# Layer 3 of a four-layer graph network in steps of one whole graph, with its start laid into the end of layer 2

## The reference

```python
Wh = (h @ W).reshape(b, n, H, HD).transpose(0, 2, 1, 3)
e1 = jnp.einsum('bhnd,d->bhn', Wh, a1)
e2 = jnp.einsum('bhnd,d->bhn', Wh, a2)
e = e1[:, :, :, None] + e2[:, :, None, :]
e = jnp.where(adj_mask[:, None, :, :] == 0, -jnp.inf, e)
e = jnp.where(e >= 0, e, ALPHA * e)
attn = jax.nn.softmax(e, axis=-1)
h_prime = jnp.einsum('bhij,bhjd->bhid', attn, Wh)
x = _layernorm(x + h_prime.transpose(0, 2, 1, 3).reshape(b, n, D_OUT))
```

## Time and profile before

| | us |
|---|---|
| median of 3 runs | 810.21 (804.77 to 817.69) |
| the profiled execution's own time | 810.46 |
| its span, first to last instruction | 808.7 |
| busy in the span: PE, DVE, ACT, POOL | 722.9, 651.0, 556.9, 447.4 |

### The profile page before, as it was taken

How to read it: one execution, slowest core, us unless ns; L and a number is a source line. 1 busy time by engine, 2 the same in 40 slices (tenths; PEclk the granted TensorE clock), 3 DMA queues, 4 the chain that set the end, 5 groups by cost and what they waited for, 6 DMA issues and landing times.

```text
span 808.7 us, 18443 instructions
## 1 busy us (share of the span) xinstructions
PE 722.9 (89%) x6397; PEld 507.2 (63%) x6397; DVE 651.0 (81%) x1754; ACT 556.9 (69%) x1141; POOL 447.4 (55%) x534
## 2 busy tenths in 40 slices
PE   3899599999689999999999999869999999999993
...
DMA packets 28893, 14.98 MB, mean 19 GB/s; under 512 B 1920, under 2 KB 28800, under 8 KB 28800
## 3 DMA queue, kind: packets, MB, share of 16 engines
...
## 4 chain that ended last, share of the span: by engine, by line
PE 51%; DVE 26%; issue 9%; ACT 9%; POOL 2%; DVEq 1%; DMA 1%; POOLq 1%; ACTq 0%
PE pair L985 10%; PE pair L1061 8%; PE bank L985 8%; ACT loopm L680 3%; DVE arena L898 3%; DVE ln L534 2%; PE bank L1149 2%; PE bank L1086 2%; DVE nmx L957 2%; PE pair L1164 2%; DVE P L937 2%; PE bank L1051 2%; PE pair L1167 2%; DVE nmx L903 2%; DVE pT L858 2%
## 5 line engine op out<-in xcount | busy, mean ns | idle before, releaser
L583 POOL TENSOR_TENSOR arena<-arena,nmx 128x1024 f32<-128x1024 f32 x64 | 121.4, 1898 | 129.1 <-DVE nmx L903 129.1
L604 POOL TENSOR_TENSOR P<-P,nmx 128x512 f32<-128x512 f32 x128 | 133.2, 1041 | 80.8 <-DVE nmx L957 78.8
L499 POOL TENSOR_TENSOR ln<-ln,neghalf 128x4 f32<-128x4 f32 x64 | 66.3, 1035 | 137.5 <-DVE ln L535 137.5
L741 ACT COPY arena<-pair 128x1024 f32<-128x1024 f32 x64 | 64.8, 1012 | 91.3 <-PE pair L985 91.3
L505 POOL TENSOR_SCALAR X<-yb,ln 128x128 f32<-128x128 f32 x256 | 119.1, 478 | 9.2 <-issue 9.2
L898 DVE TENSOR_TENSOR arena<-pair,mask 128x1024 f32<-128x1024 f32 x64 | 78.3, 1223 | 47.6 <-PE pair L1061 47.6
L937 DVE TENSOR_TENSOR P<-pair,t 128x512 f32<-128x512 f32 x128 | 87.6, 684 | 21.3 <-ACT t L761 21.1
L1061 PE MATMUL pair<-arena,hg 32*128 32x256 f32 x512 | 93.9, 444 | 2.7 <-DVE arena L898 1.7
L761 ACT ACTIVATE t<-pair 128x512 f32<-128x512 f32 x128 | 77.7, 607 | 21.9 <-PE pair L1167 21.7
L957 DVE TENSOR_REDUCE nmx<-P 128x4 f32<-128x512 f32 x128 | 85.8, 670 | 0.8
L765 ACT ACTIVATE P<-P 128x512 f32<-128x512 f32 x128 | 80.9, 632 | 3.9 <-POOL P L604 3.9
...
## 6 DMA issues: line engine op xcount, KB each, us to landing
...
```

The costliest lines, as they stand in the source:

```text
L583: nc.gpsimd.tensor_tensor(v3(P2[t % 3], HEADS), v3(P2[t % 3], HEADS), nmx2[t % 2][:].unsqueeze(2).broadcast_to([128, HEADS, N]), ALU.add)\
L604: nc.gpsimd.tensor_tensor(v3(P[u % 4][:], HQ), v3(P[u % 4][:], HQ), nmx[u % 4][:].unsqueeze(2).broadcast_to([128, HQ, N]), ALU.add)\
```

## The change

Layer 3 becomes `layer3(t)`, one graph per step, in the manner of layer 2. Scores go into `pair[t % 2]`, both banks. Scaling, maximum, reduction, addition of the row maximum, exponential and the copy of the transposes have 1024 columns each; `P`, `pT` and `t3` now lie in layer 2's buffers. The preparation has four steps (transposes of X, e, transposes of e, V) in `early(t)`, one bank; e and V are separate products, and e is split in PSUM without `er`. The addition of X moves from DVE to POOL, ahead of the scales of the batch before. Layer 3's step t stands behind layer 2's step t + 69 on every engine; it begins with t = -5, and the first scores are at t = 0. The product with V (PE) now waits for `L3_on`, the count of DVE's last product.

```diff
-def later_layers(eng, layer1, layer2, layer3, last):
+def later_layers(eng, layer1, layer2, layer3):
 
 
     every_batch(eng, layer1, before=True, after=1)
     for t in range(-4, 0):
         layer2(t)
     layer1(BATCHES + 1, 1, BATCHES // 2)
+    two_layers(layer2, layer3)
+
+
+def two_layers(layer2, layer3):
+
     for t in range(GRAPHS):
         layer2(t)
-    for u in range(UNITS):
-        layer2(GRAPHS + u)
-        layer3(-1, 1, -1, (u,))
-    for u in range(UNITS):
-        layer2(GRAPHS + UNITS + u)
-        layer3(0, 0, 0, (u,))
-    for b in range(1, BATCHES + last):
-        layer3(b, b % 2, b // 2)
+    for t in range(-AHEAD, GRAPHS + BEHIND):
+        layer2(GRAPHS + AHEAD + t)
+        layer3(t)
...
-        pair = [ctx.enter_context(nc.psum_tensor(f"pair{i}", [128, 1024], F32)) for i in range(2)]
-        bank = [pair[i // 2][:, i % 2 * 512:i % 2 * 512 + 512] for i in range(4)]
-        bank += [ctx.enter_context(nc.psum_tensor(f"bank{i}", [128, 512], F32))[:] for i in range(4, 8)]
+        pair = [ctx.enter_context(nc.psum_tensor(f"pair{i}", [128, 1024], F32)) for i in range(4)]
+        bank = [pair[i // 2][:, i % 2 * 512:i % 2 * 512 + 512] for i in range(8)]
...
-        P = [sb(f"P{i}", [128, HQ * N]) for i in range(4)]
-        pT = [sb(f"pT{i}", [128, HQ * N]) for i in range(2)]
-        xw1 = [P[s] for s in range(2)]
-        z1 = [pT[s] for s in range(2)]
+        xw1 = [sb(f"xw1{s}", [128, W]) for s in range(2)]
+        z1 = [sb(f"z1{s}", [128, W]) for s in range(2)]
...
+        t3 = kk
...
-        t3 = [sb(f"t3{i}", [128, HQ * N]) for i in range(2)]
-        nmx = [sb(f"nmx{i}", [128, HQ]) for i in range(4)]
...
-        def out_bank(b):
-            return bank[4] if b < BATCHES - 2 else bank[1]
+        def early(t):
+            return bank[5] if t < 0 else bank[6]
...
+            def layer3(t):
+                if graph(t - 1):
+                    pool.wait_ge(sem("L3_max"), t)
+                    p = P2[(t - 1) % 3]
+                    nc.gpsimd.tensor_tensor(v3(p, HEADS), v3(p, HEADS),
+                                            nmx2[(t - 1) % 2][:].unsqueeze(2).broadcast_to([128, HEADS, N]), ALU.add)\
+                      .then_inc(sem("L3_less_max"), 1)
+                b, j = t // G, t % G
+                if j == 0 and real(b - 2):
+                    pool.wait_ge(sem("L3_on"), G * (b - 1))
+                    nc.gpsimd.tensor_tensor(yb[b % 2][:], yb[b % 2][:], x_of(b - 2), ALU.add).then_inc(sem("L3_y_done"), 1)
+                if j == 3 and real(b - 2):
+                    norm_pow(pool, 3, b - 2, b % 2, b // 2)
+                    norm_scale(3, b - 2, b % 2, (0, 1))
+                if j == 0 and real(b - 3):
+                    norm_scale(3, b - 3, (b - 3) % 2, (2, 3))
+
             every_batch(pool, layer1)
-            for t in range(GRAPHS + UNITS):
-                layer2(t)
-
-            def layer3(b, s, turn):
-                for u in range(UNITS):
-                    if b == 0:
-                        layer2(GRAPHS + UNITS + u)
-                    if real(b):
-
-                        pool.wait_ge(sem("L3_max"), UNITS * b + u + 1)
-                        nc.gpsimd.tensor_tensor(v3(P[u % 4][:], HQ), v3(P[u % 4][:], HQ),
-                                                nmx[u % 4][:].unsqueeze(2).broadcast_to([128, HQ, N]), ALU.add)\
-                          .then_inc(sem("L3_less_max"), 1)
-                    if real(b - 2):
-                        if u == 5:
-                            norm_pow(pool, 3, b - 2, s, turn - 1)
-                        if u >= 6:
-                            norm_scale(3, b - 2, s, (2 * (u - 6), 2 * (u - 6) + 1))
-            every_batch(pool, layer3, after=2)
+            two_layers(layer2, layer3)
...
+            def layer3(t):
+                g = t - 4
+                if graph(g):
+                    act.wait_ge(sem("L3_pT_mm"), g + 1)
+                    need(act, sem("L3_pv_mm"), g - 1)
+                    nc.scalar.copy(pT2[g % 2], pair[2][:]).then_inc(sem("L3_pT"), 1)
+                if graph(t):
+                    act.wait_ge(sem("L3_s_mm"), t + 1)
+                    need(act, sem("L3_leaky"), t - 1)
+                    nc.scalar.mul(t3[t % 2], pair[t % 2][:], ALPHA).then_inc(sem("L3_scaled"), 1)
+                if graph(g):
+                    act.wait_ge(sem("L3_pv_mm"), g + 1)
+                    need(act, sem("L3_out_mm"), g - 1)
+                    nc.scalar.copy(oT[g % 2][:], bank[7][:, 0:2 * N]).then_inc(sem("L3_oT"), 1)
+                b, k = (t + AHEAD - 1) // G, (t + AHEAD - 1) % G
+                if real(b):
+                    if k == 0:
+                        act.wait_ge(sem("L3_xT_mm"), b + 1)
+                        need(act, sem("L3_v_mm"), b - 1)
+                        nc.scalar.copy(xT[b % 2][:], early(t - 1)).then_inc(sem("L3_xT"), 1)
+                    if k == 2:
+                        act.wait_ge(sem("L3_eT_mm"), b + 1)
+                        need(act, sem("L3_s_mm"), G * (b - 1))
+                        nc.scalar.copy(eT[b % 2][:], early(t - 1).bitcast(BF16)[:, 0:W]).then_inc(sem("L3_eT"), 1)
+                    if k == 3:
+                        act.wait_ge(sem("L3_v_mm"), b + 1)
+                        need(act, sem("L3_pv_mm"), G * (b - 1))
+                        nc.scalar.copy(vx[b % 2][:].rearrange("p (a c) -> p a c", c=HP)[:, :, 0:HD],
+                                       v3(early(t - 1), G * HEADS)).then_inc(sem("L3_v"), 1)
+                if graph(t - 2):
+                    act.wait_ge(sem("L3_less_max"), t - 1)
+                    p = P2[(t - 2) % 3]
+                    nc.scalar.activation(p, p, ACT.Exp).then_inc(sem("L3_exp"), 1)
+            later_layers(act, layer1, layer2, layer3)
...
-                    nc.vector.tensor_copy(onT, out_bank(b - 2)).then_inc(sem("L2_onT"), 1)
+                    nc.vector.tensor_copy(onT, bank[4]).then_inc(sem("L2_onT"), 1)
...
+            def layer3(t):
+                g = t - 5
+                o = bank[7][:, 2 * N:4 * N].rearrange("p (h c) -> p h c", h=HEADS)
+                if graph(g):
+                    if g % G == 0:
+                        y_slot_free(dve, 3, g // G)
+                    dve.wait_ge(sem("L3_out_mm"), g + 1)
+                    nc.vector.reciprocal(rd3[g % 2][:], o[:, :, HD]).then_inc(sem("L3_rden"), 1)
+                    dve.wait_ge(sem("L3_rden"), g + 1)
+                    nc.vector.tensor_tensor(v3(yb[g // G % 2][:, cols(g % G)], HEADS), o[:, :, 0:HD],
+                                            rd3[g % 2][:].unsqueeze(2).broadcast_to([128, HEADS, HD]), ALU.mult)\
+                      .then_inc(sem("L3_on"), 1)
+                b, k = (t + AHEAD - 1) // G, (t + AHEAD - 1) % G
+                if k == 1 and real(b):
+                    e = v3(early(t - 1)[:, 0:G * 2 * HEADS], G)
+                    dve.wait_ge(sem("L3_e_mm"), b + 1)
+                    need(dve, sem("L3_eT_mm"), b)
+                    for part in range(3):
+                        at = v3(ep[:], G)[:, :, 32 * part:32 * part + 2 * HEADS]
+                        need(dve, sem("L3_split"), 5 * b + 2 * part)
+                        nc.vector.tensor_copy(at, e).then_inc(sem("L3_split"), 1)
+                        if part < 2:
+                            dve.wait_ge(sem("L3_split"), 5 * b + 2 * part + 1)
+                            nc.vector.tensor_tensor(e, e, at, ALU.subtract).then_inc(sem("L3_split"), 1)
+                b, j = t // G, t % G
+                if graph(t - 1):
+                    p = P2[(t - 1) % 3]
+                    dve.wait_ge(sem("L3_scaled"), t)
+                    need(dve, sem("L3_pT_mm"), t - 3)
+                    nc.vector.tensor_tensor(p, pair[(t - 1) % 2][:], t3[(t - 1) % 2], ALU.max).then_inc(sem("L3_leaky"), 1)
+                if j == 3 and real(b - 2):
+                    stats_done(dve, 3, b % 2)
+                if graph(t - 1):
+                    dve.wait_ge(sem("L3_leaky"), t)
+                    need(dve, sem("L3_less_max"), t - 2)
+                    nc.vector.tensor_reduce(nmx2[(t - 1) % 2][:], v3(p, HEADS), AX.X, ALU.max, negate=True)\
+                      .then_inc(sem("L3_max"), 1)
+                if j in (1, 2) and real(b - 2):
+                    stats_nodes(dve, 3, b - 2, b % 2, (2 * j - 2, 2 * j - 1))
+            later_layers(dve, layer1, layer2, layer3)
...
-                        pe.wait_ge(sem("L2_masked"), GRAPHS)
                         need(pe, sem("L2_y_done"), b - 2)
-                    transposes(out_bank(b - 2), on[s], G).then_inc(sem("L2_onT_mm"), 1)
+                    transposes(bank[4], on[s], G).then_inc(sem("L2_onT_mm"), 1)
...
+            def layer3(t):
+                b, j = t // G, t % G
+                if graph(t):
+                    if j == 0:
+                        pe.wait_ge(sem("L3_eT"), b + 1)
+                    need(pe, sem("L3_leaky"), t - 1)
+                    for i in range(2):
```

(50 more changed lines are left out.)

179 lines of the change are left out of this document (4 added, 175 removed).

## The result

The changed kernel took 875.71 us (median of 5 runs, 871.16 to 876.69) against 810.32 us (median of 5, 804.77 to 817.69). The ratio is 1.0805, 95% interval 1.0763 to 1.0848. It is slower, as forecast, but by 65 us where the prediction had 34, and outside the range of 822 to 864. The profiled execution of the changed kernel took 871.16 us, 1.8 beside its span of 869.4.

A forecast was written before the change was run, and what follows sets the result against it. It found PE, DVE and ACT close together, and priced the new layer on DVE with its waits: 536.8 to the first maximum, 282.6 to the last and 23.1 behind give 842.5, with 1.8 more 844 us; range 822 to 864.

The forecast's parts named there:

- the wait: DVE's reciprocal at step 4b+5 waits for POOL to normalise batch b-2: 4.0 us per batch (3.9 to 4.4), 14 times.
- the early prologue: Layer 3's preparation beside layer 2's end: it gains nothing, as its small steps stand in line behind layer 2's drain.
- the batch: Sign in layer 3: a batch of four graphs takes 18 to 19.7 us if right, below 17 if wrong.
- first maximum: Start of layer 3's first maximum on DVE: 536.8 us (534 to 539), against 535.3 before.
- 13 slot waits: DVE's waits for POOL between first and last maximum: 13 of 4.0 us, 52.0 in all.
- PE's lag: DVE's reciprocal waits for PE's output in two steps per batch: 0.85 us (0 to 1.7), 15 times, 12.8 us.
- the rest of the middle: DVE's own work from first to last maximum: steps 151.2, reciprocals and products 26.4, splits 16.8, statistics 20.1, layer 2's leftovers 3.3.
- tail: From the last maximum's start to the end: 23.1 us, including a slot wait of 3.9, against 17.7 before.
- rival D: PE's granted clock falls to 0.9 while it waits, some 20 us more: 864 us; chance 0.05.
- A: The slot wait and PE's lag are the same idle time, so 12.8 us vanish: 831 us; chance 0.20.
- B: Slot wait at step 4b+5's reciprocal under about 1.3 us, POOL freeing it early: not slower, 800 or 791 us; chance 0.12.
- C: A DVE instruction sharing something with POOL is held behind its longer subtraction, up to 18 us: 862 us; chance 0.08.

The follow-up runs named there:

- warm: Changed kernel plus eleven unused bf16 products of 512 columns filling PE's pause behind the slot wait; 866.34 us, no ratio, runs from 856.91 to 870.82.
- x_last: Changed kernel with POOL's two scales issued ahead of the addition of X in step 4b+4; 845.87 us, ratio 1.0482 to the kernel before.
- yb3_out_xdve2: Changed kernel with three yb buffers, PE's output transposes earlier and the sum with X back on DVE; 807.16 us, ratio 1.0005 to the kernel before.
- pow4: Changed kernel, still two yb buffers, with all four POOL scales right behind the power in step 4b+3; 823.48 us, ratio 1.0204 to the kernel before.
- yb3: Changed kernel with a third yb buffer, so the slot wait asks for a batch one earlier; 819.04 us, ratio 1.0148 to the kernel before.
- yb3_outfirst: Changed kernel with a third yb buffer and PE's output transposes ahead of the preparation; 807.52 us, ratio 0.9981 to the kernel before.

## Why the prediction was wrong

Right in it: the wait, its place, its cause and its count (14); no gain from the early prologue; slower. Outside what it said would show it right: the waits (4.52 us for 3.9 to 4.4) and the batch (20.55 for 18 to 19.7). By its own terms:

| term | predicted | measured | error |
|---|---|---|---|
| first maximum | 536.8 | 532.7 | -4.1 |
| 13 slot waits | 52.0 | 59.9 | +7.9 |
| PE's lag | 12.8 | 27.8 | +15.0 |
| the rest of the middle | 217.8 | 222.2 | +4.4 |
| tail | 23.1 | 26.8 | +3.7 |
| span | 842.5 | 869.4 | +26.9 |

**PE's lag was mis-sized, 0.85 us a batch for 1.82** (1.28 + 0.54). This is the step that failed most. The estimate was laid out at a granted clock of 1.00, and it was good for that: warm and x_last, at 1.00, show 0.40 + 0.54 = 0.94. The other 0.9 is the clock, shown by warm. The prediction had named this as rival D (0.9 of the clock, 20 us), gave it 0.05, and treated it as an alternative to the forecast. But D follows from the forecast: the wait that it foretold makes PE stand still. A consequence belongs in the sum.

**The slot wait was 4.5 and not 4.0.** Two parts were left out. The sum with X on POOL takes 1.27 us and not 1.03: the broadcast form was the wrong row to stand in for one that reads two full operands, and the answer was inside its bounds of 0.9 and 1.45. And POOL does not start 0.08 us behind the reduction: its power and two scales, moved to the step before, still run until 704.21, 0.4 late. Only the instructions between the reduction and the release were priced, not those in front of them. The Trainium skill, GPSIMD Engine Reference, section 3.1, gave an estimate of 1.12 us for the sum with X; the trace's 1.27 lies above both that and the 1.04. As for the page's advice to leave such work on VectorE: the sum took 0.86 us there at the median, but the kernel's time was the same either way (yb3_out_xdve2).

**The tail, +3.7:** its slot wait was 5.15 instead of 3.9, and PE's last products ran at the low clock behind it.

**The rest of the middle, +4.4,** is mostly bookkeeping. The sum counts 1.14 us from a reduction's start to the next instruction, the profile counts a wait from the reduction's end, at 1.22. Over the 43 waits (13 and 30) these 0.08 us make 3.4.

**The first maximum, -4.1, is the clock of an earlier stage, and by luck it hid as much of the other errors.** The code up to there is the same in the changed kernel, x_last and warm, and those two have it at 536.5 and 537.3 us, as the 536.8 foretold. What differs is the granted clock between 200 and 260 us, long before layer 3. It is 0.77 in them and in the profile before, from which the forecast was made, and 0.86 in the profile of the changed kernel (before, then changed):

```profile
200.00:260.00 60.00, 49.40 (x272) 31.80 (x271) 36.20 (x89) 32.69 (x70) 21.36 (x28) 0.77 0.00 1
200.00:260.00 60.00, 47.70 (x308) 30.84 (x308) 38.23 (x91) 35.19 (x74) 23.23 (x27) 0.86 0.00 1
```

Every profiled kernel with 0.86 there starts layer 3 at 531.4 to 533.3, those with 0.77 at 535.3 to 537.8, and pow4, with 0.66, at 539.4. So some 4 us of the loss are hidden in the spans, and the medians' 65 us say more than the spans' 60.7.

**The rivals.** A (the wait pays for PE's lag) is wrong as it was put: the lag of 0.40 + 0.54 stands beside the slot wait in x_last and warm. But the slot wait does hide another one. Without it DVE waits 1.66 us for PE at the same place (yb3), some 22 us over 13 places, and so taking away 59.9 us of waits and 12 of clock shortened the middle by only 50.2. B needed a wait under 1.3 us, and POOL can't free the slot that early. C did not occur: between 600 and 800 us the scalar instruction of `stats_done` takes 0.17 us each time, though it had 462 ns in the mean before.

**Where the expected gain went.** Wide instructions do save DVE work. But the changed kernel added a wait of 4.5 us per batch, lost 0.9 to the clock, and gave PE a separate product of 0.91 us. With the first two taken out (yb3), layer 3's middle is still 4.0 us longer than before. Only with the output transposes moved ahead as well (yb3_outfirst) is it 9.4 us shorter, and the longer tail eats over half of that.
